# Cross attention on one core: the softmax's maximum as a bias of the exponential, one ScalarE instruction per head

## What is computed

```python
scores = jnp.einsum('bhqd,bhkd->bhqk', Q, K) / np.sqrt(D_K)
scores = jnp.where(m == 0, NEG, scores)                      # layer 0
scores = jnp.einsum('bhtd,bhsd->bhts', qh, kh) * scale + mask  # layer 1
attn = jax.nn.softmax(scores, axis=-1)
out = jnp.einsum('bhts,bhsd->bhtd', attn, vh)
```

## Time and profile before

| what | value |
|---|---|
| runs (3) | 1574.38, 1576.41 (median) and 1583.6 us |
| span of the profiled execution | 1578.5 us (no other time of that execution is given) |
| first cross attention | about 555 to 723 us of the span |
| second cross attention | about 1315 to 1482 us of the span |
| busy over the whole span | PE 77%, DVE 73%, ACT 42%, POOL 32% |
| TensorE's mean granted clock | 0.879 of full speed |

### The profile page before, as it was taken

The page is one execution under the profiler, slowest core; times in us unless marked ns, Lnnn a source line. Parts: engine busy times, 40 slices in busy tenths (PEclk is TensorE's granted clock), DMA queues, the critical chain, the costliest instruction groups (busy, mean ns, idle before and its releaser), DMA issues. The chain is left out here.

```text
span 1578.5 us, 29867 instructions
## 1 busy us (share of the span) xinstructions
PE 1208.8 (77%) x10299; PEld 990.4 (63%) x10300; DVE 1158.3 (73%) x2346; ACT 655.8 (42%) x1346; POOL 502.7 (32%) x494
## 2 busy tenths in 40 slices
PE   4889889888898789985016566588778946999687
PEld 1577676766777667774015566577667735777576
DVE  5687876777777558885945766469998984888678
ACT  3454543544444246553003332234343423555274
POOL 3212112121120035553552322135432323555222
PEclk7899999998999989995557887889988978999699
DMA  5000000100000000003322331120000002000001
GB/s 183 8 1 9 8 1 9 52 7 3 1 1 1 10 20 19 17 7 148 150 107 79 132 110 46 43 83 21 13 13 14 1 1 76 19 24 9 27 28 53
DMA packets 31080, 61.39 MB, mean 39 GB/s; under 512 B 7611, under 2 KB 20603, under 8 KB 27899
## 3 DMA queue, kind: packets, MB, share of 16 engines
q1 hardware_dynamic: 29434, 55.76, 10.0%
q0 software_dynamic: 1536, 4.20, 0.8%
HBM read 41.13 MB, written 10.42 MB: 33 GB/s over the span
## 5 line engine op out<-in xcount | busy, mean ns | idle before, releaser
L345 POOL TENSOR_TENSOR wa_rot<-wa_raw,wa_cos_sin 128x1024 f32<-128x1024 f32 x32 | 80.5, 2517 | 350.4 <-ACT wa_raw L389 348.0
L887 POOL TENSOR_TENSOR ca_z<-ca_z,ca_top 128x308 f32<-128x308 f32 x128 | 92.5, 722 | 133.9 <-DVE ca_top L1016 133.6
L639 PE MATMUL wa_scores<-wa_kt,wa_qt 128*128 128x192 f32 x512 | 121.5, 350 | 0.0
L2213 PE MATMUL re_g<-re_conv,re_w_g 128*128 128x256 f32 x512 | 112.8, 379 | 0.0
L2213 PEld LDWEIGHTS re_g<-re_conv,re_w_g 128*128 128x128 f32 x512 | 97.3, 190 | 13.2
L1143 PE MATMUL ca_turned<-ident,ca_probs 128*77 128x128 f32 x512 | 84.9, 289 | 21.0 <-ACT ca_probs L951 20.0
L959 ACT ACTIVATE ca_pth<-ca_turned 77x512 f16<-77x512 f32 x128 | 75.8, 592 | 60.3 <-PE ca_turned L1143 59.7
L1134 PE MATMUL ca_scores<-ca_km,ca_q 128*128 128x308 f32 x256 | 90.1, 435 | 5.9 <-ACT ca_q L932 5.6
L605 PE MATMUL wa_shared<-wa_wh,wa_xh 128*128 128x512 f16 x192 | 76.7, 399 | 19.8 <-ACT wa_raw L389 10.1
L1021 DVE SCALAR_TENSOR_TENSOR ca_ptl<-ca_turned,ca_pth 77x512 f16<-77x512 f32 x128 | 86.7, 677 | 2.9 <-ACT ca_pth L959 2.9
L639 PEld LDWEIGHTS wa_scores<-wa_kt,wa_qt 128*128 128x128 f32 x512 | 80.2, 197 | 13.3 <-issue 1.2
(11 more groups left out here) (310 smaller groups left out, 3924.5 us busy)
## 6 DMA issues: line engine op xcount, KB each, us to landing
ex_stage<-in_ew SPq DMA_DIRECT2D x16, 1024.0 KB, 6.8
ca_xs<-tokens SPq DMA_DIRECT2D x16, 256.0 KB, 2.4
slots<-rt_zeros SPq DMA_DIRECT2D x4, 920.0 KB
wa_w_stage<-in_wqkv SPq DMA_DIRECT2D x6, 512.0 KB, 4.5
ex_xe<-slots SPq DMA_DIRECT2D x16, 160.0 KB, 2.3
slots<-ex_y SPq DMA_DIRECT2D x15, 160.0 KB
wa_x_stage<-in_xt SPq DMA_DIRECT2D x8, 256.0 KB, 3.3
tokens<-in_x SPq DMA_DIRECT2D x1, 2048.0 KB, 10.6
```

Source lines behind the costliest of these rows:

```text
L345: pool.tensor_tensor(rot[:, r % 2], raw[:, r % 2], c, ALU.mult).then_inc(cos_done, 1)
L639: ins = pe.matmul(dst, qt[par][:, 2 * u + h, t * P:(t + 1) * P], kt[par][:, u, t * WINDOW:t * WINDOW + SPAN], start=False, stop=True)
L887: pool.tensor_tensor(z[k][:], z[k][:], top[:, k].unsqueeze(2).broadcast_to((P, UH, CTX)), ALU.subtract).then_inc(shift, 1)
L2213: ins = pe.matmul(g_bank[m][:, k], w_g[:, j, cols], conv[par][:, j], start=(j == 0), stop=(j == HT - 1))
```

## The change

`subtract` on GpSimd goes, and the maximum is taken off inside the exponential. VectorE multiplies `top` by minus the scale (into a new buffer `minus_top`, 128 x 4) right after it has found it; since it reads its own result, it waits for `maxed` first, and it is now this instruction that increments `shift`. ScalarE takes the row of `minus_top` as a bias. A bias is one number per partition, and the four heads have four different maxima, so power becomes four instructions of 77 columns; the last one increments `exped`. The scale of the scores is named `XSCALE` and is what it was.

```diff
+    XSCALE = 1.0 if additive else CD ** -0.5
+        minus_top = sb("minus_top", [P, 2, UH])
-            def subtract(b, c):
-                pool.wait_ge(maxed, b * UNITS + c + 1)
-                k = c % 2
-                pool.tensor_tensor(z[k][:], z[k][:], top[:, k].unsqueeze(2).broadcast_to((P, UH, CTX)),
-                                   ALU.subtract).then_inc(shift, 1)
                 for c in range(UNITS):
-                    if c < UNITS - 2:
-                        subtract(b, c + 2)
-                    elif after:
-                        subtract(b + 1, c + 2 - UNITS)
-            subtract(0, 0)
-            subtract(0, 1)
...
                 act.wait_ge(shift, b * UNITS + c + 1)
                 if not (first(b) and c < 2):
                     act.wait_ge(probs_t, b * UNITS + c - 1)
-                act.activation(probs[k][:], z[k][:], ACT.Exp, scale=1.0 if additive else CD ** -0.5).then_inc(exped, 1)
+                for h in range(UH):
+                    ins = act.activation(probs[k][:, h], z[k][:, h], ACT.Exp, scale=XSCALE, bias=minus_top[:, k, h:h + 1])
+                ins.then_inc(exped, 1)
...
                 dve.tensor_reduce(top[:, k], z[k][:], AX.X, ALU.max).then_inc(maxed, 1)
+                dve.wait_ge(maxed, b * UNITS + c + 1)
+                dve.tensor_scalar(minus_top[:, k], top[:, k], -XSCALE, None, ALU.mult).then_inc(shift, 1)
```

## The result

| | median us | lowest to highest | runs |
|---|---|---|---|
| before | 1576.41 | 1574.03 to 1584.84 | 5 |
| after | 1628.32 | 1619.18 to 1630.02 | 5 |

The change makes the kernel 3.0% slower: the ratio is 1.0304, with a 95% interval of 1.0263 to 1.0344. The sign was as forecast. The time was not: 1628 lies 20 us above the upper end of the range, and the loss of 52 us is more than twice the 21.8 that was worked out.

The account below looks back on a forecast made before the run. A closed TensorE-ScalarE loop, lengthened to 2.32 us, was to set the units: 1.25 us per batch over 7 steps (8.8) plus 2.1 in the last batch, 10.9 per stage, 21.8 in both, giving 1598 us; range 1586 to 1608.

Parts of the forecast that it names:

- one closed loop through two engines: Cross attentions, TensorE and ScalarE: transposes, high part, exponential, next transposes; grows from 1.70 to 2.32 us per unit.
- its cost hides under the longer loop: VectorE's negation and wait, 2.1 us per batch, fit under the derived batch of 19.45 and are costed at nothing.
- the sum's 19.47: Cross-attention batch after the change: 18.22 us plus 1.25 from the units' changed lengths.
- at the old batch length VectorE would be full: VectorE's cover is 1.2 us per batch; were the batch to stay at 18.22, VectorE would fill it entirely.
- only comes earlier: GpSimd's queue behind the removed subtraction: key masking, residual bias and square roots just run sooner, at no cost.
- the clock at nothing: TensorE's granted clock stays 1.00 despite more waiting, all but the last batch staying busier than 2.58 of 4 us.
- (a): Rival on ScalarE: the loop rules, but four exponentials cost as the PSUM row says; 1588 us, chance 0.20.
- (b): Rival on TensorE: its order is the bound and hides everything; 1576 us, chance 0.05.
- (d): Rival on VectorE: its wait on itself costs clearly more, making it the bound beside the loop; 1612 us, chance 0.05.
- (c): Rival: GpSimd's chain counts and the pieces are nearly free, deciding from four within 0.53 us; 1561 us, chance 0.03.
- The signs listed: Profile after: pieces 0.33 to 0.36 us, units 0 to 4 about 2.3, batches about 19.5, clock 1.00 in steady windows.
- I am wrong if: Refuted if units 2 and 4 stay at 1.8 us, pieces lie closer than 0.2, or VectorE has no idle time.

Follow-up runs that it names:

- the kernel without a negation and paced: Changed kernel with the maximum written negated by the reduction, four exponentials kept, GpSimd waiting for it where the subtractions stood: 1606.98 us, ratio 1.0171.
- one piece: Changed kernel with one exponential of 308 columns (first head's bias less 8) and GpSimd waiting where the subtractions stood: 1583.73 us, ratio 1.0021.
- the paced kernel: Changed kernel, GpSimd waiting for each unit's negated maximum where it used to subtract: 1607.61 us, ratio 1.0171; repeated, 1608.08 us, ratio 1.0172.
- shorter maskings alone: Changed kernel with GpSimd's key masking cut to 2 of 77 keys from the third batch on: 1604.46 us, ratio 1.0152.
- another form of the negation alone: Changed kernel with the negation done as a sign-changing reduction over one element, behind the same wait: 1606.68 us, ratio 1.0179.
- paced and without a negation: Changed kernel with one negated maximum for four heads, one exponential, no separate negation, GpSimd waiting where the subtractions stood: 1567.01 us, ratio 0.9915.

## Why the prediction was right in sign and wrong in size

**Right.** The mechanism: one closed loop through two engines that four pieces lengthen. Pieces of 0.347 (0.345 worked out), four of them 1.09 to 1.11 (1.08), a loop of 2.33 (2.32). With the loop alone, the kernel without a negation and paced, the batch is 19.61 (19.47) and the stages grow by 11.0 (562.33 to 729.04) and 14.4 (1338.40 to 1507.44), against 10.9 each. The start and length of the negation were right too (0.03 to 0.04 after the maximum, 0.17), as was what it adds to VectorE where nothing holds it (the next instruction starts 0.67 after the maximum in place of 0.38: 0.29 more, for 0.26 to 0.32 worked out), and the claim that its cost hides under the longer loop (1.0171 with and without it; the batch named beside that claim, 19.45, is the sum's 19.47), as was the remark that at the old batch length VectorE would be full (and 19.06 of 20 with one piece).

**Wrong.** The step that failed is the one on what is removed: what stands behind the subtraction on GpSimd's queue "only comes earlier", costed at nothing. It named the steps and did not ask beside which of VectorE's they would now run. The subtractions also spaced GpSimd's other steps. With them gone both maskings run one right behind the other, 2.39 us in one piece, and two instructions of VectorE in a row are held, the first of them the negation on which the next exponential waits. Respacing alone takes the batch from 21.5 to 19.85 and the ratio from 1.0304 to 1.0171; shorter maskings alone to 19.85, another form of the negation alone to 19.9. The Trainium skill has this, SBUF — State Buffer, section Who interferes with whom: VectorE and GpSimd share a pair of ports under an exclusive lock, a tensor_scalar may take it, and whichever comes second is blocked for the other's whole instruction, while a tensor_reduce never contends. The traces agree: 0.17 becomes 0.86 until the masking's end, and the reduction stays at 156 to 159 ns. So the description of the core, by which engines meet only at semaphores, is too narrow here: no semaphore ties the negation to a masking.

The second step that failed is the clock at nothing. Its own test, a steady window below 1.00, came true (0.71). TensorE is busy 2.63 of 4 us in that window and 2.58 in the row on which the cover rested, which stood at 1.00: the busy share did not tell the two apart. In the steady batches the fall came with the first failed step, since the 1.37 us that TensorE waits there is for VectorE; in the paced kernel the first stage stays at 1.00 until its last batch. The last batch, which the prediction left out of that cover and gave no price for the clock, falls without it too. In the kernel without a negation and paced, seven units of the last batch take 16.38 us in the first stage (clock 1.00 in 706 to 716) and 18.50 in the second (0.66 in 1482 to 1492), where 16.24 was worked out; this makes 2 of the 3.4 us by which the second stage grew more. The per-batch account, in us:

| | batch | from |
|---|---|---|
| before | 18.3 | |
| loop alone | 19.6 | no negation, paced |
| and the negation | 19.85 | paced |
| and what GpSimd holds | 21.1 | eight steps of after at full clock |
| and the falls of the clock | 21.5 | mean of after |

**The rivals.** (a) fell with the pieces' 0.347. (b) fell with units of 2.33. (d) put its finger on VectorE, and gave 1612, the nearest time, by luck, since its reason was wrong: the wait on itself is 0.04, and VectorE had not run out of time but was held. (c) put the turn at an exponential of 0.53: at 0.54, paced and without a negation, the kernel is indeed faster, by 13 us, close to the 15 that (c) allowed, and TensorE's wait for the exponential is 8.4 us there in place of 20.0.

The signs listed show that something is off (units 1 and 2 at 2.9, batches of 21.5) but not what, and none of the three under "I am wrong if" came: VectorE is busy 18.57 of 20, about the idle time foretold, but 2 us of this busy time per batch is being held (0.69 and 0.98 at the maskings, 0.36 at the biases). It is the longest duration of a line, not the busy share, that tells. What stays open: the 8 to 11 us by which the other runs of after exceed the profiled one, and why the kernel before with four pieces takes 7 us more in time than foreseen while its trace agrees with the expectation.

## What to carry to other kernels

A step that is taken out of an in-order queue also paced what stands behind it: write down when each later step will now run and what runs beside it on the neighbouring engine. A small instruction on the path that can be held by a neighbour is worth more than its duration; fold it into one that was not held here (a reduction that writes the sign changed), or cut the work that holds it. Before an instruction is cut in pieces, close the loop it stands in and compare that with the shortest unit, not with the engine's mean idle time.

## What the runs showed of the hardware

VectorE's tensor_scalar on as few as 128 x 4 numbers can be held for a whole GpSimd instruction (0.17 to 1.23 us), and the record shows it as a longer duration, not as idle time; a reduction of the same 128 x 4 numbers never was (159 ns at most). A scalar_tensor_tensor with both inputs in SBUF was held as well (0.42 to 0.93, with the negation alone in the kernel before). An exponential of 308 columns takes 0.540 (median) with a bias read per partition and 0.455 (mean) without one, so the bias itself costs some 0.08 us. Added waits on GpSimd, an engine busy for a quarter of the time, made a kernel 21 us faster.
